# Edge-attribute and node-feature transfers released by a count of issued scatter pairs, and one landing semaphore for the scatters

## The chip, the cores and the metric

One core of a Trainium2 chip runs the whole kernel. The metric is the device time of one execution in microseconds (us), the median over runs. The engines are TensorE (PE), VectorE (DVE), ScalarE (ACT), GpSimd (POOL) and SyncE (SP); in the trace PEld is TensorE's weight load, and a "q" behind an engine's name (POOLq, SPq) is its sequencer, which waits, counts and issues.

## What is computed

A graph layer over 50,000 nodes with 160 features and 50,000 edges, all in float32. For each edge a tensor product of the features of its node `dst` with 32 edge attributes gives 160 values; these go through a linear layer and are summed at the node `src`; each node then gets an update from its own features and its sum, and a layer norm:

```python
row, col = (edge_index[0], edge_index[1])                 # src, dst
tp = fctp_messages(node_features[col], edge_attr_tensor, W1, W2, W3, W4)
messages = tp @ Wm + bm
agg = jax.ops.segment_sum(messages, row, num_segments=N_NODES)
upd = jnp.concatenate([node_features, agg], axis=-1) @ Wu + bu
return node_features + upd
...
x = _layernorm(x + _L0_gnn_ref(x, edge_index, edge_attr_32, ...), axis=-1)
```

## The kernel before

**Edge stage.** The edges are cut into 98 groups of 512 (four tiles of 128). For each group GpSimd gathers 4 x 128 rows of node features into `xg` (L326, four indirect DMAs); TensorE transposes them into PSUM; VectorE multiplies them with the edge attributes `e_sb` into `prod` (L515, three times L527, L535, with two additions at L549); TensorE contracts `prod` with the weights (L671, L678), makes messages (L722) and sums those of equal rows within a pair of tiles (L733 on); ScalarE copies the sums out (L441); VectorE makes the row indices (L558, L568); GpSimd adds the sums into the table `agg` in HBM with four indirect DMAs with accumulation (L344). The last needs an order of its own: rows of one pair of tiles are distinct, but those of two pairs may be the same, so a pair (scatters q = 0, 1 or q = 2, 3) is issued only when all earlier scatters have landed. The first of a pair counts on the semaphore `scattered_a`, the second on `scattered_b`, 16 each.

GpSimd's slot (L349) for group s: gathers 0, 1 of group s+2, scatters 0, 1 of group s-3, gathers 2, 3 of s+2, scatters 2, 3 of s-3. The engines' loops are unrolled by four groups, with values of waits worked out in registers; the first eight slots and the last ones stand outside the loop. `hold` (L208) adds one to a semaphore that nobody reads; it gives the waits ahead of it an instruction of their own.

**Loads of the edge stage**, all on SP's queue. `e_sb` is double buffered by group. `load_es` (L215) brings four tiles (1,024 KB) for L515 and L527, `load_ev` (L227) six tiles (1,536 KB). Both wait until VectorE is through with the buffer (`multiplied`). From group 10 on `load_es`, and from group 9 on `load_ev`, also wait for the scatters of an earlier group, which no data needs: this sets *when* the load runs beside the scatters. Load_es of group n waits until the third scatter of group n-5 has landed, load_ev of group n until the first scatter of group n-4 has:

```python
sp.wait_ge(scattered_a, number(g) * 32 - 5 * 32 + 32)   # L222, load_es
sp.wait_ge(scattered_a, number(g) * 32 - 4 * 32 + 16)   # L233, load_ev
```

SP's slot issues the indices `dst_sb` (L241), the indices and row numbers `src_sb`, `row_sb` (L248, L249; 256 KB), then load_ev of the next group and load_es of the one after.

**Between the stages.** The node stage reads the features transposed, in 49 blocks of 1,024 nodes (640 KB each); sixteen of them have buffers `xT` of their own in memory that the edge stage has done with: the first eight in `prod[1]`, four in `e_sb[0]`, four in `e_sb[1]` (L134 to L136). SP waits for all of TensorE's rounds (L301), issues all sixteen (L302), waits for all scatters (L305, L306) and goes on with blocks of `agg` (L296) and the remaining features.

**Node stage.** For each block TensorE multiplies the features (L781, L785), VectorE adds the block of `agg` (L596) and takes the moments (L615, L621), ScalarE normalizes (L468), GpSimd's queue stores (L365).

Others that wait for the scatters: ScalarE before it writes `summed` again (L439, L440), VectorE before it writes `row_idx` again (L566, L567), GpSimd before each pair (L338, L339).

Of the kernel before, what the change touches and what calls it, by code (L numbers as in the profile page):

```python
# [10 lines left out]
ALU = mybir.AluOpType  # L11
# [3 lines left out]
TILES = 4  # L15
# [7 lines left out]
D = 160  # L23
# [3 lines left out]
USES = 6  # L27
ROUNDS = 7
XW = 224
MW = D + 1  # L30
# [13 lines left out]
def number(group, m=M1):  # L44
    return group[0] * m + group[1]
# [19 lines left out]
def build(nc, x, x_rows, x_t, dst_idx, src_idx, src_row, e_rep, packed, packed_first, bu, out):  # L65
    n_nodes = x.shape[0]
    n_groups = dst_idx.shape[0]
# [8 lines left out]
    with ExitStack() as ctx:  # L76
# [9 lines left out]
        def sem(name):  # L86
            return ctx.enter_context(nc.semaphore(name))
# [21 lines left out]
        e_sb = two("e_sb", [P, ET, GE])  # L109
# [3 lines left out]
        prod = two("prod", [P, NPROD, GE])  # L113
# [7 lines left out]
        summed = four("summed", [P, 2, 2 * MW])  # L121
# [9 lines left out]
        NB = GN * D // P  # L131
        an = [nodes[:, b * NB:(b + 1) * NB] for b in range(AGG_BUFS)]
        yn = [nodes[:, (AGG_BUFS + b) * NB:(AGG_BUFS + b + 1) * NB] for b in range(Y_BUFS)]
        homes = [prod[1][:, :, :], e_sb[0][:, :, :], e_sb[1][:, :, :]]  # L134
        xT = [home.rearrange("p n e -> p (n e)")[:, b * NB:(b + 1) * NB]
              for home, count in zip(homes, (8, 4, 4)) for b in range(count)]  # L136
        assert len(xT) == AHEAD
        stats = two("stats", [P, NODES_A, 6])
        mv = two("mv", [P, NODES_A, 2])
# [19 lines left out]
        es_in = [sem(f"es_in{u}") for u in range(M1)]  # L159
        ev_in = [sem(f"ev_in{u}") for u in range(M1)]  # L160
        x_gathered = [sem(f"x_gathered{u}") for u in range(M1)]

        scattered_a = sem("scattered_a")
        scattered_b = sem("scattered_b")
        xT_in = [sem(f"xT_in{b}") for b in range(AHEAD)]
        agg_in = [sem(f"agg_in{b}") for b in range(AGG_BUFS)]
        nodes_out = [sem(f"nodes_out{b}") for b in range(Y_BUFS)]
# [6 lines left out]
        rounds = sem("rounds")  # L174
# [38 lines left out]
        @block.sync  # L213
        def _(sp):
            def load_es(g):  # L215
                if at_least(g, 2):

                    sp.wait_ge(multiplied, number(g) * USES - 2 * USES + 4)
                    hold(sp, sp_passed)
                if at_least(g, 10):  # L220

                    sp.wait_ge(scattered_a, number(g) * 32 - 5 * 32 + 32)  # L222
                    hold(sp, sp_passed)
                sp.dma_start(e_sb[g[1] % 2][:, 0:4, :], e_rep[number(g), :, 0:4, :].unsqueeze(0).to_broadcast([32, 4, 4, GE])
                             ).then_inc(es_in[g[1]], 16)

            def load_ev(g):  # L227
                if at_least(g, 2):
                    sp.wait_ge(multiplied, number(g) * USES - 2 * USES + 6)
                    hold(sp, sp_passed)  # L230
                if at_least(g, 9):

                    sp.wait_ge(scattered_a, number(g) * 32 - 4 * 32 + 16)  # L233
                    hold(sp, sp_passed)
                sp.dma_start(e_sb[g[1] % 2][:, 4:ET, :], e_rep[number(g), :, 4:ET, :].unsqueeze(0).to_broadcast([32, 4, ET - 4, GE])
                             ).then_inc(ev_in[g[1]], 16)

            def load_dst(g):
                if at_least(g, 4):
                    sp.wait_ge(x_gathered[g[1]], g[0] * 64)  # L240
                sp.dma_start(dst_sb[g[1]][:, :], dst_idx[number(g), :, :]).then_inc(dst_in[g[1]], 16)  # L241

            def load_src(g):
                if at_least(g, 4):
                    sp.wait_ge(idx_step, number(g) * 2 - 6)
                    hold(sp, sp_passed)
                    sp.wait_ge(apart_done, number(g) - 3)
                sp.dma_start(src_sb[g[1]][:, :], src_idx[number(g), :, :]).then_inc(src_in[g[1]], 16)  # L248
                sp.dma_start(row_sb[g[1]][:, :], src_row[number(g), :, :].to_broadcast([P, GE])).then_inc(src_in[g[1]], 16)  # L249

            def start_table(k):
                if k >= PIECES_OUT:
                    sp.wait_ge(table_set[k % PIECES_OUT], 16 * (k // PIECES_OUT))
                cols = slice(k * SET_ROWS * D, min((k + 1) * SET_ROWS, n_rows // P) * D)
                sp.dma_start(agg.rearrange("(p r) d -> p (r d)", p=P)[:, cols],
                             start_rows[:, 0:cols.stop - cols.start]).then_inc(table_set[k % PIECES_OUT], 16)

            def slot(s):
                live = lambda d: not isinstance(s[0], int) or 0 <= number(s) + d < n_groups
                if live(4):  # L260
                    load_dst(shift(s, 4))
                if live(1):
                    load_src(shift(s, 1))
                if live(1) and at_least(s, 1):
                    load_ev(shift(s, 1))
                if live(2):
                    load_es(shift(s, 2))
                if isinstance(s[0], int) and number(s) < 4:
                    for k in range(PIECES * (number(s) + 4) // 8, PIECES * (number(s) + 5) // 8):
                        start_table(k)  # L270

            sp.dma_start(start_rows[:, 0:D], bu.to_broadcast([P, D])).then_inc(start_rows_in, 16)
            for b in range(4):
                load_dst((0, b))
            load_es((0, 0))
            load_ev((0, 0))
            load_src((0, 0))
            sp.wait_ge(start_rows_set, 1)
            for k in range(PIECES // 8):
                start_table(k)  # L280
            load_es((0, 1))
            load_ev((0, 1))
            for k in range(PIECES // 8, PIECES // 2):
                start_table(k)
            run_slots(sp, slot, 0, n_groups, 8, (n_groups - 4) // M1 * M1)

            def load_xT(n):
                if n >= AHEAD:
                    sp.wait_ge(upd_ready, n - AHEAD + 1)
                sp.dma_start(xT[n % AHEAD], x_t[n, :, :]).then_inc(xT_in[n % AHEAD], 16)  # L290

            def load_agg(n):
                if n >= AGG_BUFS:
                    sp.wait_ge(added, n - AGG_BUFS + 1)
                parts = rest if n == full else P
                sp.dma_start(an[n % AGG_BUFS][0:parts, :],  # L296
                             agg[n * GN:n * GN + parts * NODES_A, :].rearrange("(p s) d -> p (s d)", s=NODES_A)
                             ).then_inc(agg_in[n % AGG_BUFS], 16)


            sp.wait_ge(rounds, ROUNDS * n_groups)  # L301
            for n in range(AHEAD):  # L302
                load_xT(n)

            sp.wait_ge(scattered_a, 32 * n_groups)  # L305
            sp.wait_ge(scattered_b, 32 * n_groups)  # L306
            def ahead(n):

                return min(AHEAD + (n_out - AHEAD) * n // (n_out - 4), n_out)

            for n in range(n_out):
                load_agg(n)
                for m in range(ahead(max(n - 1, 0)), ahead(n)):
                    load_xT(m)

        @block.gpsimd
        def _(pool):
# [13 lines left out]
            def scatter(g, q):  # L331
                if q == 0:
                    pool.wait_ge(summed_copied, number(g) + 1)
                    pool.wait_ge(idx_step, number(g) * 2 + 2)
                if q % 2 == 0:

                    if at_least(g, 1) or q:
                        pool.wait_ge(scattered_a, number(g) * 32 + q * 8)  # L338
                        pool.wait_ge(scattered_b, number(g) * 32 + q * 8)  # L339
                    else:  # L340
                        for u in range(PIECES_OUT):
                            pool.wait_ge(table_set[u], 16 * ((PIECES - u + PIECES_OUT - 1) // PIECES_OUT))
                    hold(pool, pool_passed)
                nc.gpsimd.indirect_dma_start(  # L344
                    agg, bass.IndirectOffsetOnAxis(row_idx[g[1]][:, q:q + 1].bitcast(U32), 0),
                    summed[g[1]][:, q // 2, q % 2 * MW:q % 2 * MW + D], None, compute_op=ALU.add
                ).then_inc(scattered_b if q % 2 else scattered_a, 16)

            def slot(s):  # L349
                live = lambda d: not isinstance(s[0], int) or 0 <= number(s) + d < n_groups  # L350
# [20 lines left out]
        def _(act):  # L371
# [64 lines left out]
            def copy_summed(g):  # L436
                act.wait_ge(summed_ready, number(g) + 1)
                if at_least(g, 4):
                    act.wait_ge(scattered_a, number(g) * 32 - 96)  # L439
                    act.wait_ge(scattered_b, number(g) * 32 - 96)  # L440
                nc.scalar.activation(summed[g[1]][:, :, :], msg_ps, ACT.Copy).then_inc(summed_copied, 1)  # L441

            def slot(s):
# [43 lines left out]
        def _(dve):  # L487
# [63 lines left out]
            def rows(g, step):  # L551
                n = number(g)
# [10 lines left out]
                dve.wait_ge(idx_step, n * 2 + 1)  # L563
                dve.wait_ge(src_in[g[1]], g[0] * 32 + 32)
                if at_least(g, 4):
                    dve.wait_ge(scattered_a, n * 32 - 96)  # L566
                    dve.wait_ge(scattered_b, n * 32 - 96)  # L567
                nc.vector.tensor_tensor(row_idx[g[1]][:, :], moved[:, :], src_sb[g[1]][:, :],  # L568
                                        ALU.max).then_inc(idx_step, 1)

# [302 lines left out]
```

## Time and profile before

| | |
|---|---|
| median of 3 runs | 1829.69 us (1829.28 to 1829.8) |
| the profiled execution | 1834.27 us |
| its span in the profile | 1832.5 us |
| mean granted TensorE clock | 0.957 |
| busy in the span | PE 86%, PEld 48%, DVE 87%, ACT 49%, POOL 58% |
| DMA queues, share of 16 engines | SP's q1 57.5% (379 MB), GpSimd's q0 27.2% (109 MB) |
| chain that ended last | DMA 33% (agg<-summed 18%), issue 21%, PE 18%, DVE 14%, POOL 9% |
| VectorE busy, 1550 to 1600 us | 1.8 of 50 us |

The profile is of one execution, which took 4.6 us more than the median of the runs; 1.8 us of its time lie outside the span. Busy shares are averages over stages with different limits, so the stages are read one by one. POOL's busy time in an indirect DMA is the writing of descriptors; the data move afterwards on the DMA engines and then the semaphore tells of the landing. "Idle before" names what ended an engine's idle time: "issue" is time in which it waited for nothing that the profile shows.

### The profile page before, as it was taken

Reading aid. Unit: us, or ns where it says so; the run is one execution under the profiler, and the core shown is the slowest. Engines: PE = TensorE matmul, PEld = TensorE weight load, DVE = VectorE, ACT = ScalarE, POOL = GpSimd, SP = SyncE. Lnnn points to the kernel's source line nnn. Section 1 sums busy time; section 2 is a strip of 40 time slices with the busy share of each in tenths; the row PEclk is TensorE's granted clock in tenths of the full one; section 3 lists DMA queues with packets and bytes.
Section 4 is the critical chain, followed back from the end, with each engine's and each line's share of the span. In section 5 each row is a group of like instructions: output and inputs, shape, how many; then the busy total and the mean of one; then the engine's idle time right before and its main releaser. Section 6 shows DMA issues by size and latency. Waiting matters only on the chain.

```text
span 1832.5 us, 35242 instructions
## 1 busy us (share of the span) xinstructions
PE 1581.1 (86%) x11572; PEld 876.3 (48%) x11572; DVE 1594.1 (87%) x1825; ACT 900.5 (49%) x1721; POOL 1067.6 (58%) x837
## 2 busy tenths in 40 slices
PE   4167899999999999999999999999999999298882
PEld 2033444545444554545544454445554454276662
DVE  6276699999999999999999999999999996199994
ACT  1123444545444444555544444445554445088885
POOL 3005777777767777776777777767777774211110
PEclk8688999999999999999999999999999999699996
DMA  9996678888888888888888888888888885899994
GB/s 378 404 395 178 157 234 248 245 244 244 256 244 247 246 247 255 256 247 244 249 255 248 243 250 256 248 242 246 246 252 249 255 248 139 287 391 421 416 418 170
DMA packets 174618, 490.07 MB, mean 267 GB/s; under 512 B 48664, under 2 KB 99096, under 8 KB 149484
## 3 DMA queue, kind: packets, MB, share of 16 engines
q1 hardware_dynamic: 91980, 379.42, 57.5%
q0 software_dynamic: 82304, 109.12, 27.2%
q10 hardware_dynamic: 288, 0.95, 0.2%
q8 instruction: 24, 0.39, 0.1%
q14 instruction: 22, 0.18, 0.0%
HBM read 393.10 MB, written 96.31 MB: 267 GB/s over the span
## 4 chain that ended last, share of the span: by engine, by line
DMA 33%; issue 21%; PE 18%; DVE 14%; POOL 9%; ACT 2%; SPq 1%; POOLq 1%; DVEq 0%; ACTq 0%
DMA agg<-summed,row_idx 18%; DVE prod L527 7%; POOL agg L344 6%; DMA agg<-start_rows 5%; DMA prod<-agg 5%; DMA e_sb<-in_e_rep 4%; PE ps L671 4%; PE ps L678 3%; POOL xg L326 3%; PE ps L659 2%; DVE prod L596 2%; DVE prod L515 2%; DVE stats L615 2%; PE ps L733 1%; PE ps L722 1%
## 5 line engine op out<-in xcount | busy, mean ns | idle before, releaser
L344 POOL DMA_INDIRECT agg<-summed,row_idx x392 | 625.4, 1595 | 363.7 <-DMA agg<-summed,row_idx 183.2
L527 DVE TENSOR_TENSOR prod<-ps,e_sb 128x2048 f32<-128x2048 f32 x294 | 655.3, 2285 | 68.3 <-DMA e_sb<-in_e_rep 47.5
L678 PE MATMUL ps<-prod,packed_sb 128*32 128x512 f32 x2744 | 672.4, 607 | 0.8 <-ACT S_sb L398 0.8
L326 POOL DMA_INDIRECT xg<-in_x_rows,dst_sb x392 | 415.7, 1060 | 187.7 <-issue 113.6
L671 PE MATMUL ps<-prod,packed_sb 128*32 128x512 f32 x2352 | 396.3, 603 | 0.0
L535 DVE TENSOR_TENSOR prod<-ps,e_sb 128x3072 f32<-128x3072 f32 x98 | 328.3, 3350 | 0.0
L515 DVE TENSOR_TENSOR prod<-ps,e_sb 128x2048 f32<-128x2048 f32 x98 | 223.8, 2283 | 49.8 <-issue 32.0
L659 PEld LDWEIGHTS ps<-packed_sb,spread 128*128 128x128 f32 x1176 | 127.8, 143 | 221.8 <-issue 104.5
L441 ACT ACTIVATE summed<-ps 128x644 f32<-128x644 f32 x98 | 69.4, 708 | 330.9 <-PE ps L736 234.0
L659 PE MATMUL ps<-packed_sb,spread 128*128 128x128 f32 x1176 | 174.5, 286 | 51.3 <-issue 28.4
L468 ACT ACTIVATE prod<-prod,shift_n,rstd 128x160 f32<-128x160 f32 (+1 forms) x392 | 166.6, 507 | 40.8 <-DVE shift_n L608 40.8
L549 DVE TENSOR_TENSOR prod<-prod 128x1024 f32<-128x1024 f32 x196 | 186.6, 952 | 0.0
L386 ACT ACTIVATE spread<-xg 128x1536 f32<-128x1536 f32 x98 | 144.6, 1476 | 77.2 <-DMA xg<-in_x_rows,dst_sb 69.9
L722 PE MATMUL ps<-wc_s,S_sb 128*128 128x160 f32 x784 | 180.9, 311 | 1.2 <-ACT S_sb L398 1.2
L671 PEld LDWEIGHTS ps<-prod,packed_sb 128*32 128x32 f32 x2352 | 78.2, 109 | 206.1 <-issue 192.6
L678 PEld LDWEIGHTS ps<-prod,packed_sb 128*32 128x32 f32 x2744 | 127.2, 109 | 94.4 <-issue 92.6
L723 PE MATMUL ps<-wc_v,V_sb 97*128 97x160 f32 x784 | 170.9, 298 | 0.0
L416 ACT ACTIVATE apart<-row_sb,neg_src 128x256 f32<-128x256 int32 x392 | 166.2, 500 | 0.0
L667 PE MATMUL ps<-A_sb,packed_sb 64*128 64x512 f32 x392 | 112.9, 652 | 61.2 <-DVE prod L527 61.0
L392 ACT ACTIVATE A_sb<-ps 128x512 f32<-128x512 f32 x98 | 58.4, 596 | 216.4 <-PE ps L651 172.7
L722 PEld LDWEIGHTS ps<-wc_s,S_sb 128*128 128x128 f32 x784 | 124.8, 189 | 83.4 <-issue 81.3
L398 ACT ACTIVATE S_sb<-ps 128x512 f32<-128x512 f32 x98 | 58.6, 598 | 186.7 <-PE ps L678 186.7
(62 smaller groups left out, 1702.4 us busy)
## 6 DMA issues: line engine op xcount, KB each, us to landing
e_sb<-in_e_rep SPq DMA_DIRECT2D x98, 1536.0 KB
e_sb<-in_e_rep SPq DMA_DIRECT2D x98, 1024.0 KB
agg<-start_rows SPq DMA_DIRECT2D x49, 640.0 KB, 15.1
prod<-agg SPq DMA_DIRECT2D x48, 640.0 KB, 10.3
out<-prod POOLq DMA_DIRECT2D x48, 640.0 KB, 7.7
row_sb<-in_src_row SPq DMA_DIRECT2D x98, 256.0 KB
prod<-in_x_t SPq DMA_DIRECT2D x25, 640.0 KB, 12.0
e_sb<-in_x_t SPq DMA_DIRECT2D x24, 640.0 KB, 12.7
```

The source lines that it names most:

```text
L326: nc.gpsimd.indirect_dma_start(xg[g[1] % 2][:, q, :], None, x_rows, bass.IndirectOffsetOnAxis(dst_sb[g[1]][:, q:q + 1].bitcast(U32), 0)).t ...
L344: nc.gpsimd.indirect_dma_start(agg, bass.IndirectOffsetOnAxis(row_idx[g[1]][:, q:q + 1].bitcast(U32), 0), summed[g[1]][:, q // 2, q % 2 * ...
L468: last = nc.scalar.activation(y[0:parts, cols], y[0:parts, cols], ACT.Identity, bias=shift_n[v][0:parts, q:q + 1], scale=rstd[v][0:parts, ...
L515: nc.vector.tensor_tensor(prod[g[1] % 2][:, 0:4, :], ps[:, t_bank(g, 0), :].unsqueeze(1).to_broadcast([P, 4, GE]), e_sb[g[1] % 2][:, 0:4, ...
L527: nc.vector.tensor_tensor(prod[g[1] % 2][:, 4 + 4 * i:8 + 4 * i, :].rearrange("p (a b) e -> p a b e", b=2), ps[:, t_bank(g, 1 + i), :].uns ...
L535: nc.vector.tensor_tensor(prod[g[1] % 2][:, 16:22, :].rearrange("p (f i) e -> p f i e", f=2), ps[:, first:first + 2, :].unsqueeze(2).to_br ...
L549: nc.vector.tensor_tensor(total, total, more, ALU.add).then_inc(parts_added, 1)
L659: last = nc.tensor.transpose(ps[:, t_bank(g, 1 + i), q * P:(q + 1) * P], spread[:, q, i * P:(i + 1) * P], ident_sb[:, :])
L671: return nc.tensor.matmul(ps[32 * i:32 * i + 32, V_BANK, :], w, prod[g[1] % 2][:, tile, :], start=start, stop=stop)
L678: return nc.tensor.matmul(ps[32 * quarter:32 * quarter + 32, S_BANK, :], w[:, 32 * half:32 * half + 32], prod[g[1] % 2][:, tile, :], start ...
L722: nc.tensor.matmul(to, S_sb[g[1] % 2][:, q * P:(q + 1) * P], wc_s[:, :], start=True, stop=False)
L723: last = nc.tensor.matmul(to, V_sb[g[1] % 2][:, q * P:(q + 1) * P], wc_v[:, :], start=False, stop=True)
```

## The change

The two kinds of e_sb loads, and the sixteen early loads of features, are released by a new semaphore `pairs_issued`. GpSimd's program adds one to it right behind the second scatter of each pair. The thresholds name the same pair as before, but its issue in place of its first scatter's landing (load_es: second pair of group n-5; load_ev: first pair of group n-4). The sixteen feature loads start when the first product buffer is free, two or three with each pair from the 190th of 196 on; their buffers come in another order for that. `scattered_a` and `scattered_b` become one semaphore `scattered`, so each wait for the scatters is one wait in place of two.

```diff
-        homes = [prod[1][:, :, :], e_sb[0][:, :, :], e_sb[1][:, :, :]]
+        homes = [e_sb[0][:, :, :], e_sb[1][:, :, :], prod[1][:, :, :]]
...
-              for home, count in zip(homes, (8, 4, 4)) for b in range(count)]
+              for home, count in zip(homes, (4, 4, 8)) for b in range(count)]
...
-        scattered_a = sem("scattered_a")
-        scattered_b = sem("scattered_b")
+        scattered = sem("scattered")
+        pairs_issued = sem("pairs_issued")
...
-                    sp.wait_ge(scattered_a, number(g) * 32 - 5 * 32 + 32)
+                    sp.wait_ge(pairs_issued, number(g) * 2 - 5 * 2 + 2)
...
-                    sp.wait_ge(scattered_a, number(g) * 32 - 4 * 32 + 16)
+                    sp.wait_ge(pairs_issued, number(g) * 2 - 4 * 2 + 1)
...
-            sp.wait_ge(rounds, ROUNDS * n_groups)
             for n in range(AHEAD):
+                if n == 0:
+                    sp.wait_ge(multiplied, USES * (n_groups - 1))
+                if n == 4:
+                    sp.wait_ge(multiplied, USES * n_groups)
+                if n == 8:
+
+                    sp.wait_ge(rounds, ROUNDS * n_groups)
+                if n in (0, 2, 4, 6, 8, 10, 13):
+                    sp.wait_ge(pairs_issued, 2 * n_groups - 6 + min(n // 2, 6))
                 load_xT(n)
 
-            sp.wait_ge(scattered_a, 32 * n_groups)
-            sp.wait_ge(scattered_b, 32 * n_groups)
+            sp.wait_ge(scattered, 16 * TILES * n_groups)
...
-                        pool.wait_ge(scattered_a, number(g) * 32 + q * 8)
-                        pool.wait_ge(scattered_b, number(g) * 32 + q * 8)
+                        pool.wait_ge(scattered, number(g) * 64 + q * 16)
...
-                    summed[g[1]][:, q // 2, q % 2 * MW:q % 2 * MW + D], None, compute_op=ALU.add
-                ).then_inc(scattered_b if q % 2 else scattered_a, 16)
+                    summed[g[1]][:, q // 2, q % 2 * MW:q % 2 * MW + D], None, compute_op=ALU.add).then_inc(scattered, 16)
+                if q % 2:
+                    pool.sem_inc(pairs_issued, 1)
...
-                    act.wait_ge(scattered_a, number(g) * 32 - 96)
-                    act.wait_ge(scattered_b, number(g) * 32 - 96)
+                    act.wait_ge(scattered, number(g) * 64 - 192)
...
-                    dve.wait_ge(scattered_a, n * 32 - 96)
-                    dve.wait_ge(scattered_b, n * 32 - 96)
+                    dve.wait_ge(scattered, n * 64 - 192)
```

## Rows read from the trace of the kernel before

**Rows 1.** Busy time by stretches: length, busy of each engine, clock, DMA share, GB/s.
```profile
500.00:1000.00 500.00, 477.39 (x3463) 250.18 (x3465) 481.67 (x304) 248.50 (x441) 357.87 (x272) 1.00 0.86 250
...
1600.00:1700.00 100.00, 87.29 (x757) 69.98 (x758) 96.05 (x454) 81.58 (x205) 11.84 (x22) 0.97 0.99 406
```

**Rows 2.** Groups by line of VectorE, 217.5 to 1532.7 us.
```profile
L527 DVE TENSOR_TENSOR prod<-ps,e_sb 128x2048 f32<-128x2048 f32 x265 | 590.7, 2285 | 42.1 <-DMA e_sb<-in_e_rep 27.4 <-issue 5.1 <-PE ps L678 4.5
...
L568 DVE TENSOR_TENSOR row_idx<-moved,src_sb 128x4 int32<-128x4 f32 x89 | 14.5, 163 | 21.6 <-DMA agg<-summed,row_idx 11.1 <-DVE moved L558 6.1 <-issue 4.3
```

**Rows 3.** Groups by line of GpSimd, 217.5 to 1532.7 us.
```profile
L344 POOL DMA_INDIRECT agg<-summed,row_idx x356 | 568.8, 1598 | 262.0 <-DMA agg<-summed,row_idx 142.4 <-issue 110.0 <-ACT summed L441 8.2
L326 POOL DMA_INDIRECT xg<-in_x_rows,dst_sb x350 | 374.1, 1069 | 106.6 <-issue 103.3 <-DMA agg<-summed,row_idx 3.0 <-DVE row_idx L568 0.3
```

**Rows 4.** Timeline, 802 to 819 us: SP's issue, and each pair's first scatter.
```profile
802.66 0.58 SPq L235 DMA_DIRECT2D e_sb<-in_e_rep  x1
...
803.53 1.61 POOL L344 DMA_INDIRECT agg<-summed,row_idx  x1 [1.72 <-DMA agg<-summed,row_idx]
...
811.23 1.61 POOL L344 DMA_INDIRECT agg<-summed,row_idx  x1 [1.59 <-DMA agg<-summed,row_idx]
...
818.61 1.61 POOL L344 DMA_INDIRECT agg<-summed,row_idx  x1 [0.31 <-issue]
```

**Rows 5.** Waits of L209, 802.0 to 802.7 us: ns min/median/max, first to last start.
```profile
L209 SPq EVENT_SEMAPHORE  x1: 17/17/17, 802.4 to 802.4; - x1
```

**Rows 6.** Busy time by stretches, in two neighbouring cycles.
```profile
802.66:804.00 1.34, 1.34 (x15) 1.17 (x17) 1.34 (x1) 0.00 (x0) 0.47 (x1) 1.00 0.17 56
804.00:808.60 4.60, 4.60 (x40) 1.80 (x43) 4.60 (x3) 2.52 (x6) 3.74 (x3) 1.00 1.00 339
808.60:810.50 1.90, 1.90 (x19) 1.06 (x12) 1.28 (x4) 1.90 (x4) 0.98 (x1) 1.00 0.93 185
...
811.50:814.60 3.10, 2.99 (x20) 1.07 (x18) 3.10 (x3) 1.27 (x4) 2.79 (x2) 1.00 1.02 333
```

**Rows 7.** Timeline of GpSimd, 1546 to 1575 us: the first scatter of each pair.
```profile
1546.26 1.54 POOL L344 DMA_INDIRECT agg<-summed,row_idx  x1 [2.70 <-DMA agg<-summed,row_idx]
...
1552.21 1.54 POOL L344 DMA_INDIRECT agg<-summed,row_idx  x1 [2.57 <-DMA agg<-summed,row_idx]
...
1563.08 1.54 POOL L344 DMA_INDIRECT agg<-summed,row_idx  x1 [7.48 <-issue]
...
1573.38 1.54 POOL L344 DMA_INDIRECT agg<-summed,row_idx  x1 [6.91 <-DMA agg<-summed,row_idx]
```

**Rows 8.** Busy time by stretches, in the pair of 1546.26 us.
```profile
1550.20:1551.40 1.20, 1.20 (x15) 0.77 (x17) 0.00 (x0) 0.39 (x1) 0.00 (x0) 1.00 0.72 68
```

**Rows 9.** L323 (GpSimd's register step for its next slot's first wait), 655 to 658 us.
```profile
L323 POOLq FUSED_REGOPS  x1: 46/46/46, 656.3 to 656.3; - x1
```

**Rows 10.** Timeline of GpSimd, 655 to 658 us: the scatters ahead of that step.
```profile
655.93 1.61 POOL L344 DMA_INDIRECT agg<-summed,row_idx  x1 [0.79 <-issue]
657.84 1.58 POOL L344 DMA_INDIRECT agg<-summed,row_idx  x1 [0.30 <-issue]
```

**Rows 11.** Timeline of GpSimd and SP, 186 to 197 and 217 to 224 us.
```profile
186.92 1.61 POOL L344 DMA_INDIRECT agg<-summed,row_idx  x1 [0.68 <-DVE moved L558]
...
187.49 0.55 SPq L235 DMA_DIRECT2D e_sb<-in_e_rep  x1
...
196.82 1.61 POOL L344 DMA_INDIRECT agg<-summed,row_idx  x1 [3.80 <-DMA agg<-summed,row_idx]
...
217.58 1.61 POOL L344 DMA_INDIRECT agg<-summed,row_idx  x1 [0.30 <-issue]
...
221.29 0.60 SPq L235 DMA_DIRECT2D e_sb<-in_e_rep  x1
...
224.00 1.61 POOL L344 DMA_INDIRECT agg<-summed,row_idx  x1 [0.31 <-issue]
```

**Rows 12.** Timeline of SP, 1595 us: the first loads of agg.
```profile
1595.05 1.27 SPq L296 DMA_DIRECT2D prod<-agg  x3
```

## Prediction

> **What bounds the kernel now.** I read the busy time by stretches first [rows 1]. There are an edge stage to about 1545 us, a hole of 50 us in which VectorE is idle while the last scatters land, and the node stage from 1600 us. In the edge stage (the row of 500 to 1000 us) VectorE is busy 96% and TensorE 95%. In the node stage the DMA engines are 99% busy at 406 GB/s: it is bound by transfers, and the change does not touch it.
>
> VectorE's groups for 217.5 to 1532.7 us, the stretch in which the edited triggers act, come next [rows 2]. Its idle time is 42.1 us before L527 (27.4 of it ended by an e_sb landing) and 21.6 us before L568. So this engine could give some 60 us of 1315 and no more.
>
> The other engine to look at is GpSimd [rows 3]. For each group it issues four scatters and four gathers, 1.6 and 1.07 us each with 0.3 between them, and in this stretch 142.4 us of its idle time were ended by landings of agg. Busy and idle together (568.8 + 262.0 + 374.1 + 106.6 = 1311.5) are the whole stretch: GpSimd never rests except for landings. 356 scatters are 178 pairs, so one pair takes (1532.7 - 217.5) / 178 = 7.39 us and a group of two pairs 14.78 us. Without landings a pair would take 2 x 1.6 + 2 x 1.07 + 4 x 0.3 = 6.5 us. So GpSimd with its landings and VectorE share the bound, and a landing that comes 1 us later costs nearly 1 us per pair.
>
> **The cycle in detail.** A pair starts at 803.53, the next at 811.23 and the next at 818.61; just ahead of the first SP issues the six-tile load (L235), at 802.66 [rows 4]. SP's wait had ended at 802.4 [rows 5], so some 0.2 us lie between. The DMA engines' share is 0.17 until 804.0 (1.34 us from issue to data), then 1.00 for 4.6 us at 339 GB/s, then 0.93 at 185 GB/s: scatter and gather rows [rows 6]. For the four-tile load (L224) the full stretch is 3.1 us, from 811.5 to 814.6; scatter rows and the loads of the indices and of row_sb come behind it. So today a load, triggered by a landing, runs over the first half of the *next* pair, and that pair lands when it is through: the next scatter starts 2.6 us after the load's end (808.6 to 811.23) and 4.0 us after (814.6 to 818.61, with row_sb in between).
>
> A pair alone on the queues is the reference. It starts at 1546.26 [rows 7], the second scatter's data move from 1550.2 to 1551.4 [rows 8], and the next pair starts at 1552.21 [rows 7]: 6.0 us, of which 2.0 pass from the second scatter's first data to the next pair.
>
> **The change, part by part.**
>
> 1. The trigger of the two e_sb loads (89 groups for L235, from group 9; 88 for L224, from group 10). It moves from the landing of a pair's first scatter to a count that GpSimd's sequencer raises behind the pair's second scatter. When is that? The instruction behind a second scatter in the program is L323 of the next slot. It runs at 656.3 [rows 9], with the first scatter's work begun at 655.93 and the second's only at 657.84 [rows 10]. So the sequencer hands the indirect transfers to a queue and goes on; the count will rise some 0.4 us after the pair *starts*, not when its descriptors are written. The Trainium skill (Advanced Engine Details and Errata, Engine Queue Depths) gives GpSimd a queue eight deep, and by that rule the count could even run ahead of the pair's start; the trace agrees that it runs ahead.
>
>    The load's data then start 0.4 + 0.2 + 1.34 = 2.0 us (rounded up) into the pair and lie over the second scatter's, which alone would move at 3.9 to 5.1 us [rows 8]. For L235: load until 2.0 + 4.6 = 6.6, then the tail of 2.0 (the second scatter alone [rows 8]) to 2.6 us (both and the gathers [rows 6]): 8.6 to 9.2. For L224: until 2.0 + 3.1 = 5.1, then a tail of 2.0 to 4.0: 7.1 to 9.1. I take 8.8 and 7.5 (here row_sb no longer stands ahead of the second scatter in full, so nearer to the low end): 16.3 us per group, ends 15.7 and 18.3. Against 14.78 that is 1.5 us, over 89 groups 135 us; at the low end 82.
>
>    The trace has its own trials of this. Before group 9 the loads are not held back. The pair of 186.92 had L235 issued at 187.49, 0.6 us into it, as the change will have it, and took 9.9 us [rows 11]; the pair of 217.58 had it issued 3.7 us into it and took 6.4 [rows 11]. The first had a row_sb load ahead of it (256 KB, 0.8 us at 339 GB/s), so 9.1 without.
>
> 2. What waits behind the longer pair: the loads themselves come early enough (landing 7 us into the pair, while the group's scatters are four groups behind), but GpSimd's gathers sit in the same order as its scatters, so VectorE follows at 16.3 us per group. Its 27.4 us of e_sb waits [rows 2] are replaced by longer ones.
>
> 3. One landing semaphore: the wait of L567 goes on VectorE. The idle before L568 is 21.6 / 89 = 0.24 us per group for four waits and a register step, so at most 0.1 us per group, 9 us, and only if VectorE sets the pace; by my reading it does not, so 0. ScalarE's L440 is the same, and ScalarE is busy under half the time [rows 1]. On GpSimd the count adds one semaphore instruction per pair, hidden under the first scatter's 1.6 us; uncovered, 196 times the 17 ns of such an instruction [rows 5] are 3 us.
>
> 4. The drain. Now x_t's sixteen loads are issued together after TensorE's last round, and the pairs that meet them take 10.9 us (from 1552.21) and 10.3 us (from 1563.08) instead of 6 [rows 7]. From the pair of 1532.7, where the gated loads end, to the first agg load at 1595.05 [rows 12] it is 62.3 us. After the change two loads go out with each pair from the second of these eight pairs on (three with the last two). Two are 1.31 MB, 3.2 us at 406 GB/s [rows 1]: 2.0 + 3.2 + 2.0 = 7.2 for five pairs, 36; one clean pair of 6; a pair with three loads 8.8; the last, to its landing, 8.1. Sum 58.9, a gain of 3 us. With landings held longer it is a loss of up to 10; the floor of 6 per pair gives a gain of 13. SP has nothing else to do there. The new places of xT cost nothing: same sizes, same queue.
>
> Sum on the profiled execution: 1834.27 + 135 - 3 = 1966; it lies 4.6 us over the median of the runs, so 1962, and I say 1960.
>
> **Rivals.**
>
> *The count rises late, or the scatters slip past the load.* If it rose at the end of the second scatter's descriptors (3.5 us into the pair), loads would move from 5.1 us on, behind the landing, and end 3.3 us into the next pair: the 217.58 case, 6.4 us [rows 11]. GpSimd then has room (6.5 per pair of its own work) and VectorE is the bound: of its 42.1 us before L527 about 33 go (0.1 us per group is its own step), with 6 from L567 and 4 from the drain: 1829.7 - 43 = 1787. For it speaks the second case of [rows 11]; against it, where L323 stands [rows 9, 10]. The other way to this time is that the DMA engines serve the scatter's rows in between. The Trainium skill (DMA: Bandwidth & Descriptors, Queues, rings and completion order) says that each engine takes turns between queues after every packet; if the scatter's rows took their turns at once this would be the outcome. Against it: in the pair of 1563.08, whose rows meet the x_t loads, the interval is 10.3 us [rows 7]. Together 0.25.
>
> *Nothing that can be told.* The load lies 1.5 us later relative to its pair but the first scatter lands before it, and two tails of 2.0 with no row_sb make 8.2 + 6.9: with a slightly earlier count the group is back at 14.8, the drain gives a few us: 1826 to 1833. 0.03.
>
> *Slower, the forecast*: the mechanism is the second scatter held behind a load that its own pair set off; it decides as soon as the load's data start before 3.9 us into the pair. 0.72.
>
> **How the numbers follow.** A measurement of this kernel can tell about 0.2% (3.7 us) from no change. Slower 0.72, faster 0.25, same 0.03. The slower case alone spans 1880 (15.4 us per group, a few tenths below the low end) to 2025 (17.1, within the high end, which would need every tail at its longest). To leave out no more than 2 in 10 the range must reach the other sign too: 1785 to 2025.
>
> **What would show it.** In the changed profile: SP's e_sb issues 0.5 to 0.7 us after a pair's first scatter starts (right) or 3.7 us after (wrong); the interval of pairs alternating near 8.8 and 7.5 (right) or 6.4 to 7.3 (wrong); GpSimd's idle before L344 ended by agg landings well over 142 us; VectorE's busy share in 500 to 1300 us near 87% against 96%; the first agg load near 1727 us against 1595; the node stage unchanged. If the share of VectorE stays at 96% or rises, step 1 is wrong.

## The result and the profile after

The changed kernel takes 2093.28 us (median, 2087.73 to 2100.27) against 1829.74 in the same session: ratio 1.143, 95% interval 1.139 to 1.148. It is slower, as forecast, but by 264 us and not by 130, and above the range of 1785 to 2025.

The page of the kernel after, its parts 1 and 5 (busy time; costliest groups):

```profile
PE 1654.6 (79%) x11572; PEld 888.2 (42%) x11572; DVE 1593.6 (76%) x1825; ACT 903.7 (43%) x1721; POOL 1043.4 (50%) x837
...
L349 POOL DMA_INDIRECT agg<-summed,row_idx x392 | 625.6, 1596 | 644.2 <-DMA agg<-summed,row_idx 543.8
L532 DVE TENSOR_TENSOR prod<-ps,e_sb 128x2048 f32<-128x2048 f32 x294 | 655.3, 2284 | 327.4 <-DMA e_sb<-in_e_rep 321.3
```

VectorE's work is the same 1594 us in a longer span. What grew is idle time: GpSimd waits 543.8 us for landings of agg, and VectorE 321.3 us for e_sb.

Groups by line for the stretch that answers to [rows 2] and [rows 3], 217.5 to 1791.7 us, first GpSimd, then VectorE:

```profile
L349 POOL DMA_INDIRECT agg<-summed,row_idx x357 | 570.2, 1597 | 550.4 <-DMA agg<-summed,row_idx 495.8 <-issue 54.6
```

```profile
L532 DVE TENSOR_TENSOR prod<-ps,e_sb 128x2048 f32<-128x2048 f32 x267 | 595.1, 2284 | 301.9 <-DMA e_sb<-in_e_rep 301.9
...
L572 DVE TENSOR_TENSOR row_idx<-moved,src_sb 128x4 int32<-128x4 f32 x89 | 14.8, 166 | 15.6 <-DVE moved L563 9.7
```

Landing waits went from 142.4 to 495.8 us, waits for e_sb from 27.4 to 301.9. The idle before row_idx fell from 21.6 to 15.6 us: that is the wait that was merged away, the 6 us (0.07 per group) that the prediction bounded by 9, here hidden. (With the memset's count of experiments 4 and 5 it is 15.6 us with one landing semaphore and 21.6 with two.)

The cycle, timeline of GpSimd and of SP (start, duration, what it is), to be read beside [rows 4]:

```profile
803.49 1.61 POOL L349 DMA_INDIRECT agg<-summed,row_idx  x1 [2.98 <-DMA agg<-summed,row_idx]
805.41 1.58 POOL L349 DMA_INDIRECT agg<-summed,row_idx  x1 [0.31 <-issue]
...
812.53 1.61 POOL L349 DMA_INDIRECT agg<-summed,row_idx  x1 [2.93 <-DMA agg<-summed,row_idx]
...
821.42 1.61 POOL L349 DMA_INDIRECT agg<-summed,row_idx  x1 [2.77 <-DMA agg<-summed,row_idx]
...
804.00 0.55 SPq L234 DMA_DIRECT2D e_sb<-in_e_rep  x1
813.02 0.54 SPq L223 DMA_DIRECT2D e_sb<-in_e_rep  x1
...
814.94 0.64 SPq L248 DMA_DIRECT2D row_sb<-in_src_row  x1
```

The new count itself, L353 in 803 to 805 us:

```profile
L353 POOLq EVENT_SEMAPHORE  x1: 17/17/17, 803.7 to 803.7; - x1
```

The pair begins at 803.49, the count rises at 803.7, SP issues at 804.00, and only at 805.41 does GpSimd begin the second of the two scatters that the count calls issued. The pairs take 9.04 and 8.89 us.

Busy time by stretches of the same cycle (last two columns: DMA share, GB/s), to be read beside [rows 6]:

```profile
804.00:805.40 1.40, 1.40 (x12) 0.59 (x6) 1.40 (x3) 0.48 (x1) 1.10 (x1) 1.00 0.30 61
805.40:810.10 4.70, 4.70 (x37) 2.90 (x35) 1.79 (x3) 2.18 (x6) 3.58 (x3) 1.00 0.94 327
...
814.30:818.10 3.80, 3.18 (x24) 0.91 (x23) 3.80 (x3) 2.10 (x5) 3.04 (x3) 1.00 1.00 286
818.10:820.40 2.30, 2.30 (x22) 2.13 (x25) 2.30 (x2) 0.00 (x0) 0.55 (x1) 1.00 1.10 267
```

By these rows the six-tile load keeps the DMA engines full from 1.9 to 6.6 us of its pair and the four-tile load from 1.8 to 5.6. In the trace's packets their last pieces end a little later, at 7.1 and 5.9 us, and the next pair starts 2.0 and 3.0 us after that.

**Both scatters wait, not only the second.** The DMA queues of the same pair, first 805.3 to 809.1 us, then 809.1 to 811.5 (packets, MB, share of the engines' time; q1 is SP's queue, q0 GpSimd's):

```profile
q1 hardware_dynamic: 106, 1.30, 100.7%
...
q0 software_dynamic: 373, 0.38, 74.6%
q1 hardware_dynamic: 38, 0.27, 28.5%
```

In the kernel before, the pair of 803.53 in 804.0 to 808.3 us, and the first scatter of the pair alone on the queues (1546.26) in 1548.2 to 1549.7 us:

```profile
q1 hardware_dynamic: 121, 1.49, 102.0%
...
1548.20:1549.70 1.50, 1.50 (x13) 0.76 (x6) 0.00 (x0) 0.00 (x0) 1.44 (x1) 1.00 0.57 55
```

Alone, the first scatter's rows (packets of 640 bytes) move 2.1 to 3.1 us into its pair. Beside a load nothing of GpSimd's queue moves until the load is nearly through: the 256 rows of both scatters moved from 809.14 to 811.38, the load's pieces from 805.34 to 810.58, and in the kernel before from 808.39 to 810.03. In 170 of the 178 pairs of the steady stretch it is so; in the other eight the first scatter came ahead of the load, and those pairs were no shorter. So the pair lands some time after its load is through, and this time hardly changed. From a load's first data to the next pair it was 7.2 and 7.1 us before (804.02 to 811.23, 811.51 to 818.61) and is 7.2 and 7.1 after (805.35 to 812.53, 814.36 to 821.42); means over the steady stretch are 7.4 and 7.0 before, 7.1 and 6.8 after. What changed is where in the pair the load's data start: 0.2 to 0.3 us into it before, 1.9 after.

Where the 260.4 us of span come from: GpSimd's pairs 11 to 188 (from the pair of 216.0 to that of 1791.7) take 8.85 us each instead of 7.39, so 1575.7 - 1315.2 = 260.5 us. From there to the first agg load it is 62.9 us instead of 62.3, ahead of the stretch 1.6 us less, and in the node stage 0.9 more. All of it is the pair's interval. The granted clock in 500 to 1000 us fell from 1.00 to 0.94, in a stretch in which TensorE now idles for 15% of the time and GpSimd's pairs start on landings; no run tests the clock by itself.

### The profile page after: what moved, and what is told of

Its sections match the earlier page's. It is cut to its first block, busy times and chain, and to the rows that moved or that the text cites. A ratio compares the mean times of both kernels' runs of the same rounds, so it can differ in the third digit from the quotient of the medians.

```text
span 2092.9 us, 35258 instructions
## 1 busy us (share of the span) xinstructions
PE 1654.6 (79%) x11572; PEld 888.2 (42%) x11572; DVE 1593.6 (76%) x1825; ACT 903.7 (43%) x1721; POOL 1043.4 (50%) x837
## 4 chain that ended last, share of the span: by engine, by line
DMA 66%; issue 23%; DVE 4%; POOL 4%; POOLq 1%; PE 1%; SPq 1%; ACT 1%; ACTq 0%; DVEq 0%
DMA agg<-summed,row_idx 54%; DMA prod<-agg 5%; DMA agg<-start_rows 4%; POOL agg L349 3%; DVE prod L600 2%; DVE stats L619 1%; DMA xg<-in_x_rows,dst_sb 1%; DMA e_sb<-in_e_rep 1%; DVE mv L625 1%; PE ps L785 0%; POOL xg L332 0%; DVE prod L532 0%; POOLq L208 0%; ACT prod L473 0%; DMA start_rows<-in_bu 0%
## 5 line engine op out<-in xcount | busy, mean ns | idle before, releaser
L349 POOL DMA_INDIRECT agg<-summed,row_idx x392 | 625.6, 1596 | 644.2 <-DMA agg<-summed,row_idx 543.8
L532 DVE TENSOR_TENSOR prod<-ps,e_sb 128x2048 f32<-128x2048 f32 x294 | 655.3, 2284 | 327.4 <-DMA e_sb<-in_e_rep 321.3
L682 PE MATMUL ps<-prod,packed_sb 128*32 128x512 f32 x2744 | 712.5, 631 | 0.8 <-ACT S_sb L404 0.8
L332 POOL DMA_INDIRECT xg<-in_x_rows,dst_sb x392 | 391.4, 998 | 187.9 <-issue 117.9
L675 PE MATMUL ps<-prod,packed_sb 128*32 128x512 f32 x2352 | 429.7, 648 | 0.0
L671 PE MATMUL ps<-A_sb,packed_sb 64*128 64x512 f32 x392 | 134.9, 770 | 258.8 <-DVE prod L532 258.8
L671 PEld LDWEIGHTS ps<-A_sb,packed_sb 64*128 64x128 f32 x392 | 33.2, 206 | 282.9 <-DVE prod L532 232.6
```

The source lines that it names most:

```text
L332: nc.gpsimd.indirect_dma_start(xg[g[1] % 2][:, q, :], None, x_rows, bass.IndirectOffsetOnAxis(dst_sb[g[1]][:, q:q + 1].bitcast(U32), 0)).t ...
L349: nc.gpsimd.indirect_dma_start(agg, bass.IndirectOffsetOnAxis(row_idx[g[1]][:, q:q + 1].bitcast(U32), 0), summed[g[1]][:, q // 2, q % 2 * ...
L532: nc.vector.tensor_tensor(prod[g[1] % 2][:, 4 + 4 * i:8 + 4 * i, :].rearrange("p (a b) e -> p a b e", b=2), ps[:, t_bank(g, 1 + i), :].uns ...
L671: nc.tensor.matmul(ps[:, t_bank(g, 4 + f), :], w3_sb[64 * f:64 * f + 64, :], A_sb[g[1] % 2][64 * f:64 * f + 64, :], start=True, stop=True) ...
L675: return nc.tensor.matmul(ps[32 * i:32 * i + 32, V_BANK, :], w, prod[g[1] % 2][:, tile, :], start=start, stop=stop)
L682: return nc.tensor.matmul(ps[32 * quarter:32 * quarter + 32, S_BANK, :], w[:, 32 * half:32 * half + 32], prod[g[1] % 2][:, tile, :], start ...
```

## The experiments

Two theories stood against each other at first: that the load lies over its own pair's second scatter and holds its landing (the prediction's), and that the time is lost elsewhere in the change, in the drain, the merged semaphore or the count itself. Each time is compared with the kernel before on the same chip: 1839.9 us for experiments 1 to 4, 1844.3 for 5 to 8, and 1842.5, a single run, for 9 and 10. Line numbers move with the edits: L223, L224 and L225 are the four-tile load, L234, L235 and L236 the six-tile load. A pair's mean interval can be read from the count of scatters in 500 to 1300 us: 1600 / count.

**1. The triggers alone.**

```diff
 # kernel before, plus the semaphore pairs_issued and its count behind the second scatter
-                    sp.wait_ge(scattered_a, number(g) * 32 - 5 * 32 + 32)
+                    sp.wait_ge(pairs_issued, number(g) * 2 - 5 * 2 + 2)
-                    sp.wait_ge(scattered_a, number(g) * 32 - 4 * 32 + 16)
+                    sp.wait_ge(pairs_issued, number(g) * 2 - 4 * 2 + 1)
```

> The kernel before, with only the two e_sb loads released by the count of issued pairs; two landing semaphores and the old drain stay. Theory (a load released behind its pair's start lies over that pair's own second scatter and holds its landing): the pair takes 8.8 to 8.9 us on average as in the whole change, 2080 to 2105 us. Rival (the single landing semaphore, or the early feature loads, or both cost the time): within 10 us of before, 1820 to 1840.

Measured: 2100.22 us, ratio 1.141 (1.137 to 1.145), that is 260 us of loss against 264 for the whole change. The two changed waits are the loss.

**2. The drain alone.** The feature buffers' order and their release by the count, on the kernel before.

```diff
-            sp.wait_ge(rounds, ROUNDS * n_groups)
             for n in range(AHEAD):
+                if n == 0:
+                    sp.wait_ge(multiplied, USES * (n_groups - 1))
...
+                if n in (0, 2, 4, 6, 8, 10, 13):
+                    sp.wait_ge(pairs_issued, 2 * n_groups - 6 + min(n // 2, 6))
```

> The kernel before with only the drain's part: the order of the feature buffers and their release by the count; e_sb loads wait for landings, two landing semaphores. Theory: the pair keeps 7.4 us, the stretch from the 189th pair to the first agg load keeps 62 to 63 us, 1825 to 1835 us. Rival (the drain carries part of the loss): over 1845.

Measured: 1838.87 against 1839.85, ratio 0.999 (0.998 to 1.001): nothing. (The range expected was written from the 1829.7 us of another session.) The sixteen loads do start 12 us earlier, yet the pairs take 7.6 to 9.4 us where three took 10 and the rest 6, and the last lands 8.7 us after its start and not 5.4; from the pair of 1534.7 to the first agg load it is 64.6 us, 2 more than expected.

**3. The count 1.2 us earlier.**

```diff
 # the whole change; at GpSimd's wait for the landings, ahead of the pair
-                    hold(pool, pool_passed)
+                    pool.sem_inc(pairs_issued, 1)
                 nc.gpsimd.indirect_dma_start(agg, ...).then_inc(scattered, 16)
-                if q % 2:
-                    pool.sem_inc(pairs_issued, 1)
```

> The whole change, but GpSimd's sequencer counts a pair right behind its wait for the landings, ahead of its first scatter, so about 1.2 us earlier. Theory (what matters is where the load's data lie against the scatters): data start 0.7 us into the pair and end before the second scatter's turn, the pair takes 7.5 to 7.9 us, 1835 to 1900 us. Rival (a release by GpSimd's count is slow in itself, or one semaphore is): 2050 or more.

Measured: 1893.64, ratio 1.029 (1.026 to 1.033), at the upper end of what was expected. The same count, the same semaphores, SP's issue now 0.5 us *ahead* of the pair, and four fifths of the loss are gone. The theory's reason is only half right: the data do start 0.8 us into the pair, but they don't end before the second scatter's turn. In the pair of 807.22 the six-tile load moves from 808.02 to 813.13 and the rows of both scatters from 812.31 to 814.04, behind it. The pair is shorter because the load ends 1 us earlier in it.

**4. The count behind GpSimd's own work.**

```diff
 # the whole change; mark is a [1, 1] tile; the added wait and its hold only order the memsets
                 if q % 2:
-                    pool.sem_inc(pairs_issued, 1)
+                    if at_least(g, 1) or q > 1:
+                        pool.wait_ge(pairs_issued, number(g) * 2 + q // 2)
+                        hold(pool, pool_passed)
+                    nc.gpsimd.memset(mark[:, :], 0.0).then_inc(pairs_issued, 1)
```

> The whole change, but the count is raised by a memset of one element queued on GpSimd itself behind the second scatter, so it comes when the descriptors are written, about 3.9 us into the pair, not at dispatch. Theory: the load's data start at 5.2 us, behind the pair's second scatter, and are over 3.5 us into the next; the pair takes 6.9 to 7.3 us and VectorE sets the pace: 1785 to 1825 us. Rival one (the memset and its gap burden GpSimd, which is never idle): 1835 to 1870. Rival two (any count is slow): 2050 or more.

Measured: 1800.70 us against 1839.85, ratio 0.979 (0.976 to 0.982): faster than both kernels. Timeline of its GpSimd and SP:

```profile
802.42 2.09 POOL L350 DMA_INDIRECT agg<-summed,row_idx  x1 [0.30 <-issue]
804.81 1.58 POOL L350 DMA_INDIRECT agg<-summed,row_idx  x1 [0.30 <-issue]
805.83 0.59 POOL L357 MEMSET mark<- 1x1 f32 x1
...
810.42 1.61 POOL L350 DMA_INDIRECT agg<-summed,row_idx  x1 [1.35 <-DVE row_idx L576]
...
806.65 0.54 SPq L224 DMA_DIRECT2D e_sb<-in_e_rep  x1
```

The memset ends at 806.42, SP issues 0.2 us later, 4.2 us into the pair. The groups of the same run, GpSimd in 217.5 to 1505 us:

```profile
L350 POOL DMA_INDIRECT agg<-summed,row_idx x356 | 606.5, 1704 | 210.7 <-issue 114.2 <-DVE row_idx L576 91.1 <-DMA agg<-summed,row_idx 5.1
...
L357 POOL MEMSET mark<- 1x1 f32 x178 | 106.6, 599 | 0.0
```

Landing waits are 5.1 us in place of 142.4 before and 495.8 after. GpSimd now waits for VectorE (91.1 us before L350): the pairs alternate 6.4 and 8.0, 14.45 us per group. The memsets' 106.6 us of busy time cost GpSimd nothing that shows: most of a memset lies beside the scatter (805.83 is inside 804.81 to 806.39), and from a second scatter's start to the next gather it is 1.88 us (804.81 to 806.69), against 1.89 in the kernel after (805.41 to 807.30). VectorE is busy 98% in 500 to 1000 us (489.95 of 500), against 96%.

**5. The same count with the old drain.** Experiment 1 with the memset's count.

> The kernel before (two landing semaphores, old drain) with the two e_sb loads released by the count that the memset behind the second scatter raises. Theory: VectorE sets the pace at 14.5 us per group, the drain is that of before: 1800 to 1812 us, within 10 us above the version with the whole change around it. Rival (the drain or the single semaphore gave most of the 39 us): over 1825.

Measured: 1811.97 against 1844.26, ratio 0.982 (0.979 to 0.986), 11 us above experiment 4 where 10 was the limit expected. The triggers give most; the ratios leave 0.4% for the early feature loads and the merged semaphore together. In the profiles the stretch from the 189th pair to the first agg load is 62.0 us here (1509.6 to 1571.6) and 54.6 in experiment 4 (1505.2 to 1559.8). So the early feature loads, worth nothing in experiment 2, shorten that stretch by 7 us when the count tells of finished work.

**6. The count between the two scatters.**

```diff
 # as in 4, but queued behind the first scatter of a pair
-                if q % 2:
+                if q % 2 == 0:
```

> The whole change with the count raised by the one-element memset queued between a pair's two scatters, so it comes about 2 us into the pair and the load's data start 3.4 us into it, just ahead of the second scatter's. Theory (the held second scatter lands when the load is through): the pair's interval grows with the load's start, from 8.85 us at 1.9 us to 10.0 to 10.6 at 3.4, in all 2290 to 2400 us. Rival (the loss falls the later the load starts): below 2093.

Measured: 2232.2 us in one run (before: 1844.3). Worse than the whole change, as the theory wants and against the rival, but below the theory's 2290. 169 scatters in 500 to 1300 us are 9.5 us per pair, not 10.0 or more. In its trace the first scatter's rows have moved by 3.1 us, ahead of the load, so only the second's are behind it, and the time from the load's end to the next pair is 1.6 to 1.7 us, not 2.0 to 2.9. Timeline of its GpSimd:

```profile
806.90 1.61 POOL L350 DMA_INDIRECT agg<-summed,row_idx  x1 [4.02 <-DMA agg<-summed,row_idx]
807.92 0.63 POOL L357 MEMSET mark<- 1x1 f32 x1
808.82 1.58 POOL L350 DMA_INDIRECT agg<-summed,row_idx  x1 [0.27 <-issue]
...
815.86 1.61 POOL L350 DMA_INDIRECT agg<-summed,row_idx  x1 [2.85 <-DMA agg<-summed,row_idx]
```

**7. row_sb behind the other load.** This asks why the L223 pair took 8.74 us and not the 7.5 forecast.

```diff
 # the whole change; SP's slot
-                if live(1):
-                    load_src(shift(s, 1))
                 if live(1) and at_least(s, 1):
                     load_ev(shift(s, 1))
+                if live(1):
+                    load_src(shift(s, 1))
```

> The whole change with one order turned round on SP's queue: the loads of src_sb and row_sb are issued behind the six-tile load instead of behind the four-tile load. Theory (the L224 pair takes 8.8 us and not 7.5 because row_sb's rows stand ahead of the second scatter): L224 pairs fall to 7.4 to 7.9 us, L234 pairs rise to 9.4 to 9.9, the sum stays within 0.5 us of 17.7. Rival (the L224 pair is long for another reason, such as the tail behind any load): L224 pairs stay over 8.4 us.

Measured: 2094.61 us in one run. Over the pairs of the steady stretch the L223 pairs fall from 8.74 to 7.98 us, just outside the 7.4 to 7.9 expected, and the L234 pairs rise from 8.99 to 9.82; the sum is 17.8 (17.7). row_sb costs 0.8 us in whichever of the two pairs it is issued. It does not stand whole ahead of a scatter, as the theory words it: in the kernel after its rows move from 818.24 to 819.97, among those of both scatters (817.70 to 820.10). Two neighbouring pairs:

```profile
796.11 1.61 POOL L349 DMA_INDIRECT agg<-summed,row_idx  x1 [1.32 <-DMA agg<-summed,row_idx]
...
805.85 1.61 POOL L349 DMA_INDIRECT agg<-summed,row_idx  x1 [3.62 <-DMA agg<-summed,row_idx]
...
813.78 1.61 POOL L349 DMA_INDIRECT agg<-summed,row_idx  x1 [1.51 <-DMA agg<-summed,row_idx]
```

**8 and 9. One trigger alone.** Experiment 1 with only one of its two edits.

> The kernel before with only the four-tile load (L224) released by the sequencer's count; the six-tile load waits for its landing. Theory: the L224 load lies over its own pair (8.7 to 9.0 us). The six-tile load of the pair after is released by a landing and keeps about 7.4: mean pair 7.9 to 8.2 us, 1920 to 1985 us. Rival (the loss is that of the six-tile load): within 15 us of before.

> The kernel before with only the six-tile load (L235) released by the sequencer's count; the four-tile load waits for its landing. Theory: the L235 load lies over its own pair (9 us); the four-tile load, released by the third scatter's landing, starts its data 5.2 us into its pair and runs into the next pair, where the six-tile load then queues behind it, as the run with the other trigger alone showed the other way round: mean pair 8.1 to 8.6 us, 1955 to 2050 us, so the two parts together cost less than their sum. Rival (the parts add up: 263 less the 164 of the other): 1925 to 1945.

Measured, one run each: 2008.38 us against 1844.3 with the four-tile load alone (+164), and 2097.33 against 1842.5 with the six-tile load alone (+255). Both missed: the first is above its range, the second far above, and equal to both triggers together. In the trace of the first the six-tile load, released by a landing, is issued 3.6 us into one pair (809.29 in the pair of 805.66) and moves until 816.47, well into the next. There the four-tile load, released by the count, moves behind it, from 815.59 to 820.14, and the pair takes 10.0 us:

```profile
812.07 1.61 POOL L345 DMA_INDIRECT agg<-summed,row_idx  x1 [0.31 <-issue]
...
822.08 1.61 POOL L345 DMA_INDIRECT agg<-summed,row_idx  x1 [3.89 <-DMA agg<-summed,row_idx]
...
809.29 0.58 SPq L236 DMA_DIRECT2D e_sb<-in_e_rep  x1
812.41 0.54 SPq L225 DMA_DIRECT2D e_sb<-in_e_rep  x1
```

Timeline of the second, GpSimd and SP:

```profile
799.43 1.61 POOL L345 DMA_INDIRECT agg<-summed,row_idx  x1 [5.16 <-DMA agg<-summed,row_idx]
...
805.85 1.64 POOL L345 DMA_INDIRECT agg<-summed,row_idx  x1 [0.30 <-issue]
...
817.24 1.61 POOL L345 DMA_INDIRECT agg<-summed,row_idx  x1 [5.19 <-DMA agg<-summed,row_idx]
...
803.20 0.54 SPq L225 DMA_DIRECT2D e_sb<-in_e_rep  x1
...
805.22 0.39 SPq L250 DMA_DIRECT2D row_sb<-in_src_row  x1
806.10 0.55 SPq L236 DMA_DIRECT2D e_sb<-in_e_rep  x1
```

The pair of 799.43 is free of loads and lands early, so it releases the four-tile load by its landing at 3.8 us; the next pair, at 805.85, releases the six-tile load by its count at 0.25 us. Both loads and row_sb meet one pair: it takes 11.4 us, the other 6.4, together the 17.8 of the whole change. The two triggers don't add up. What counts is how much is already queued when a scatter's rows arrive, and a landing that comes early moves the other load into the way.

**10. The six-tile load in two.**

```diff
-                sp.dma_start(e_sb[g[1] % 2][:, 4:ET, :], ...).then_inc(ev_in[g[1]], 16)
+                for lo, hi in ((4, 7), (7, ET)):
+                    sp.dma_start(e_sb[g[1] % 2][:, lo:hi, :], ...).then_inc(ev_in[g[1]], 16)
```

(VectorE waits for 32 per group on `ev_in`.)

> The whole change with the six-tile load issued as two loads of three tiles, so its pieces are 6 KB a partition in place of 12. Theory (the scatter's rows wait for what the other queue has already been given, so the bytes count and not the size of a piece): the L234 pairs stay at 8.8 to 9.2 us, 2080 to 2110 us. Rival (the scatter's rows get a turn after each piece of the load, so the wait halves with the piece): L234 pairs of 8.4 us or less, 2045 or less.

Measured: 2141.07 us in one run; L235 pairs of 9.50 us, outside both expectations, on the far side from the rival. In the trace the first scatter's rows move between the two loads and the second's behind the second load. In the pair of 816.87, whose loads run from 818.72 to 824.56, the first scatter's 128 rows move from 821.41 to 822.71 and the second's from 823.71 to 825.01. Until a load was nearly through no row was let in, whatever the size of its pieces; then one scatter was. That makes the pair longer and not shorter: with the rows in between, the loads end 7.9 us into the pair in place of 7.0, and the next pair follows 1.6 us later in place of 2.0. The DMA queues of that pair in 819.0 to 821.3 us and in 821.4 to 822.7:

```profile
q1 hardware_dynamic: 109, 0.67, 106.8%
...
q0 software_dynamic: 144, 0.08, 48.0%
q1 hardware_dynamic: 62, 0.28, 60.1%
```

Whether the scatter gets in because a load ends, or because its rows came before the second load's, this run does not tell apart.

## Why the prediction was right in kind and wrong in size

**Step 1, where the count falls: right.** Forecast 0.4 us into the pair, from L323's place in the queue; measured 0.2 to 0.3, and the load's data from 1.9 us against 2.0. Experiments 3, 4 and 6 move little but the count and shift the time to 1894, 1801 and 2232 us: the place of the load's data in the pair decides. The mechanism was right in kind but too narrow. The prediction has only the second scatter behind the load and lets the first land ahead of it; in the trace the rows of both wait, before the change as after it. That the load's start at 1.9 us catches the first scatter too (alone its rows move from 2.1 us) did not lengthen the pair, as the eight pairs show in which it slipped through.

**Step 1, the six-tile load's pair: right.** 8.8 forecast, 8.99 measured. Two errors nearly cancel here: the load's last pieces end at 7.0 us on average, not 6.6, and the tail behind them is 2.0, not 2.2.

**Step 1, the four-tile load's pair: this term failed.** I took 7.5 from between 7.1 and 9.1, "nearer to the low end", because row_sb would no longer stand ahead of the second scatter. It is 8.74. The sum was a load until 5.1 us and a tail of 2.4; measured over the steady stretch it is 5.8 and 2.9. Two parts: the load's pieces take 3.9 us and not 3.1 (they took 3.8 before the change too; the 3.1 of [rows 6] ends where other rows come in beside the last pieces); and row_sb, issued 2.4 us into the pair (814.94), still moves among the scatters' rows, just as before, which experiment 7 prices at 0.8 us. The prediction's own row for this tail, the 4.0 us between 814.6 and 818.61 [rows 4, 6], was the better witness: SP issues row_sb behind the four-tile load in its slot's order, and that order did not change. Simpler still, its rows give 7.2 and 7.1 us from a load's first data to the next pair (804.0 to 811.23, 811.5 to 818.61); from data at 2.0 us that is 9.2 and 9.1, the high end of 18.3 and 0.6 above what was measured. The group is 17.70 us and not 16.3; 1.4 x 89 = 125 of the 133 us that were missing. At the high end of its own bound, 18.3, the sum would have held it; I cut the range at 17.1 although I had a row for the longer tail.

**Step 2: right.** VectorE's idle time follows GpSimd's; its busy share in 500 to 1000 us is 80% (398.52 of 500) and not 87%, by the same factor.

**Step 3: right.** The merged wait is worth 6 us on VectorE (21.6 to 15.6 us) and nothing that shows where GpSimd sets the pace.

**Step 4, the drain: a gain of 3 us forecast, a loss of 0.6 measured.** Five pairs with two loads take 7.6 to 7.9 us and not 7.2, the pair with three 9.8 and not 8.8, and the last lands 8.5 us after its start, not 8.1. The term that was short is the loads' own time. In the pair of 1797.69 it is 1.3 us to their data, 4.3 for the two loads (1798.99 to 1803.25) and 2.1 behind them, where I had 2.0 + 3.2 + 2.0; the 3.2 came from the rate of the node stage.

**The rivals.** The late count was given 0.25 and a time of 1787. It was not what the change does, but its arithmetic was sound: experiment 4 builds it and gives 1801 on a chip where the kernel before takes 1840, a ratio of 0.979 against 1787 / 1829.7 = 0.977. The other way to that time, rows that take their turns at once, is refuted for these loads: until a load was nearly through no row of a scatter moved, with pieces of 12, 8 and 6 KB. Turns between whole loads are not refuted; experiment 10 shows one.

## What to carry to other kernels

A count that GpSimd's program raises behind an indirect DMA tells that the sequencer has handed it over, not that its descriptors are written. Where a count is to set the phase of a large load, raise it by a small instruction on the engine itself, behind the DMAs, and look in the timeline at what lies under the load's first data; here that is worth 14% between the two ways to count, and 2% against the landing. And price a moved load with everything that its queue issues behind it: row_sb, which no edit touched, cost 0.8 us per group. The cheapest forecast was at hand: measure the time from a load's first data to the next pair in the kernel before, and shift it.

## What the runs showed of the hardware

- GpSimd's sequencer is ahead of its indirect DMAs: the count behind the second scatter rises 0.2 us after the *first* one's start and 1.7 us ahead of the second's (803.7; 803.49 and 805.41). A memset in the same place is ordered by the engine: it runs from 805.83 to 806.42, about the end of the second scatter's descriptors (806.39).
- A scatter of 128 rows that meets a running load on the other queue moves when that load is nearly through, with pieces of 12, 8 and 6 KB a partition (the after and `ev_in_two` traces). How many queued loads it waits for varies. In experiment 2's drain the rows of both scatters (1545.97 to 1547.60) moved behind both loads of their pair (1542.26 to 1546.69); in the kernel before, with eight loads issued by 1557.7, the second scatter's rows moved from 1559.06 to 1561.32, behind the second load of them. What sets it is open.
- The pair's mean interval against the start of the load's data in it: 7.39 us at 0.2, 7.75 at 0.85, 8.85 at 1.9, 9.54 at 3.3, and 7.22 (VectorE's pace) at 5.2 to 5.6, when the pair's own rows have moved. Of the places tried the worst is just ahead of the second scatter's rows, and 2 us later is the best.
- Of two triggers that set the phase of one queue, the six-tile load's alone cost as much as both (255 and 260 us), which I had not expected.
